# Attention stage of a two-layer perceiver block on one core: the out products of rows 0 to 511 are issued between the first softmax steps of rows 512 to 1023

## The reference

```
# _L0_attn_ref, on b=16, t=64, 16 heads
scores = einsum('bhqd,bhkd->bhqk', q, k) * scale
attn = softmax(scores + causal_mask)
out = einsum('bhqk,bhkd->bhqd', attn, v)
x = x + out @ wo + bo
# _L0_ffn_ref
xr = mu_r * x + (1 - mu_r) * x_prev ; xk = mu_k * x + (1 - mu_k) * x_prev
r = sigmoid(xr @ W_r) ; k = square(relu(xk @ W_k))
x = x + r * (k @ W_v)
```

## Time and profile before

| what | value |
|---|---|
| runs | 1480.25, 1472.99, 1463.63 us |
| profiled execution, time | 1465.62 us |
| its span | 1463.8 us, granted TensorE clock 0.959 on average |
| PE busy | 1343.8 us, 92% |
| DVE busy | 923.2 us, 63% |
| ACT busy | 557.0 us, 38% |
| POOL busy | 496.7 us, 34% |
| PE on the chain of waits | 69% |
| DVE on the chain of waits | 23% |

### The profile page before, as it was taken

The page is one execution under the profiler, slowest core; times in us unless marked ns, Lnnn a source line. Parts: engine busy times, 40 slices in busy tenths (PEclk is TensorE's granted clock), DMA queues, the critical chain, the costliest instruction groups (busy, mean ns, idle before and its releaser), DMA issues.

```text
span 1463.8 us, 28428 instructions
## 1 busy us (share of the span) xinstructions
PE 1343.8 (92%) x11066; PEld 812.0 (55%) x11066; DVE 923.2 (63%) x2273; ACT 557.0 (38%) x1149; POOL 496.7 (34%) x424
## 2 busy tenths in 40 slices
PE   6889999999999999999999867989898999889998
PEld 3458888888874444444445445444444455655554
DVE  6858888888743323500667586585998366676761
ACT  3446777777762222000133225142314234233430
POOL 3003100000048335733416220154690049996300
PEclk9979999999999999999999977999999999779999
DMA  6111232211112111311101110021320001110000
GB/s 187 39 50 64 83 99 75 64 64 61 53 44 87 57 57 58 73 57 57 31 29 32 57 30 2 25 92 58 115 97 27 1 2 60 60 59 1 1 22 36
DMA packets 50429, 79.19 MB, mean 54 GB/s; under 512 B 13808, under 2 KB 14320, under 8 KB 50304
## 3 DMA queue, kind: packets, MB, share of 16 engines
q1 hardware_dynamic: 47296, 70.83, 15.2%
q0 software_dynamic: 1920, 6.29, 1.4%
q10 hardware_dynamic: 1088, 0.37, 0.1%
HBM read 75.38 MB, written 2.10 MB: 53 GB/s over the span
## 4 chain that ended last, share of the span: by engine, by line
PE 69%; DVE 23%; issue 4%; ACT 3%; DMA 1%; POOL 0%; DVEq 0%; POOLq 0%; ACTq 0%
PE psum L635 40%; PE psum L968 7%; PE psum L877 4%; PE psum L644 4%; PE psum L1292 4%; PE psum L867 2%; DVE big L2210 2%; PE psum L980 1%; DVE stats L2181 1%; PE psum L650 1%; DVE big L1969 1%; PE psum L860 1%; DVE nw L1947 1%; PE psum L1280 1%; DVE nw L1948 1%
## 5 line engine op out<-in xcount | busy, mean ns | idle before, releaser
L2958 POOL TENSOR_TENSOR ring_hi<-stage,small 128x512 bf16<-128x512 f32 x128 | 139.6, 1101 | 618.0 <-DVE big L2226 373.6
L635 PE MATMUL psum<-y_mem,ring_hi 128*128 128x512 bf16 x896 | 269.8, 383 | 6.0 <-issue 2.1
L635 PE MATMUL psum<-ring_hi,y_mem 128*128 128x512 bf16 x576 | 171.8, 385 | 5.9 <-DVE ring_lo L2539 3.3
L635 PE MATMUL psum<-y_mem,ring_lo 128*128 128x512 bf16 x448 | 171.1, 382 | 0.0
L1413 ACT ACTIVATE big<-psum 128x400 bf16<-128x400 f32 (+2 forms) x232 | 124.2, 547 | 79.8 <-PE psum L635 40.0
L635 PEld LDWEIGHTS psum<-y_mem,ring_hi 128*128 (+1 forms) x896 | 87.0, 99 | 108.2 <-issue 8.7
L2961 POOL TENSOR_TENSOR ring_lo<-stage,ring_hi 128x512 bf16<-128x512 f32 x96 | 118.2, 1231 | 0.0
L635 PE MATMUL psum<-ring_lo,y_mem 128*128 128x512 bf16 x352 | 116.7, 383 | 1.2 <-DVE ring_lo L2651 1.2
L1413 ACT ACTIVATE y_mem<-psum 128x512 bf16<-128x512 f32 x64 | 37.0, 596 | 175.6 <-PE psum L644 175.2
L635 PEld LDWEIGHTS psum<-ring_hi,y_mem 128*128 128x128 bf16 x576 | 56.8, 99 | 71.9 <-issue 7.4
L2308 DVE TENSOR_TENSOR side<-psum,ybuf 128x512 f32<-128x512 f32 x32 | 22.1, 692 | 107.1 <-ACT ybuf L1640 107.1
(11 more groups left out here) (261 smaller groups left out, 2883.3 us busy)
## 6 DMA issues: line engine op xcount, KB each, us to landing
big<-in_ctx_dram SPq DMA_DIRECT2D x64, 200.0 KB
stage<-in_L_xattn_Wff_dram SPq DMA_DIRECT2D x12, 1024.0 KB, 5.3
ybuf<-in_L_ffn_W_fc_dram SPq DMA_DIRECT2D x16, 256.0 KB, 2.7
ybuf<-in_L_ffn_W_proj_dram SPq DMA_DIRECT2D x16, 256.0 KB, 2.9
stage<-in_L_ffn_W_fc_dram SPq DMA_DIRECT2D x4, 1024.0 KB, 5.3
stage<-in_L_ffn_W_proj_dram SPq DMA_DIRECT2D x4, 1024.0 KB, 5.4
stage<-in_L_xattn_Wout_dram SPq DMA_DIRECT2D x3, 1024.0 KB, 5.2
stage<-in_L_attn_W_qkv_dram SPq DMA_DIRECT2D x3, 1024.0 KB, 5.2
```

Of the source, the lines that this page charges most:

```text
L635: ins = pe.matmul(bank, l, r, start=n == 0, stop=n == len(passes) - 1)
L2958: pool.tensor_tensor(hi[:, k], src[:, k], zero, ALU.add).then_inc(pool_part, 1)
```

## The change

Two things change. In the main program, on PE, ACT and DVE alike, the softmax of half 1 is opened ahead of the rest of `attn_out(0, 0)`; its first four steps are issued one by one with the four out products between them, and only its last eight steps have three steps of `rest` behind each. The filler of 20 ahead of the out products is gone, and one of 24 stands behind the last softmax step. On POOL the split of a piece is issued as hi, lo, hi, lo, each with a wait for the one before, where it was hi, hi, lo, hi, lo, hi, lo, lo with waits on the piece before.

```diff
@@ PE @@
-            filler(0, 20)
-            run(ending)
-            abreast(soft(0, 1), rest, 3, False)
+            softmax = soft(0, 1)
+            abreast(itertools.islice(softmax, 4), ending, 1)
+            abreast(softmax, rest, 3, False)
+            filler(0, 24)
             run(rest)
@@ POOL, split @@
                     for k in range(KC):
                         pool.tensor_tensor(hi[:, k], src[:, k], zero, ALU.add).then_inc(pool_part, 1)
-                        if k:
-                            pool.wait_ge(pool_part, parts[0] + k)
-                            pool.tensor_tensor(lo[:, k - 1], src[:, k - 1], hi[:, k - 1], ALU.subtract)
-                    parts[0] += KC
-                    pool.wait_ge(pool_part, parts[0])
-                    pool.tensor_tensor(lo[:, KC - 1], src[:, KC - 1], hi[:, KC - 1], ALU.subtract).then_inc(pool_split, 1)
+                        parts[0] += 1
+                        pool.wait_ge(pool_part, parts[0])
+                        ins = pool.tensor_tensor(lo[:, k], src[:, k], hi[:, k], ALU.subtract)
+                        if k < KC - 1:
+                            ins.then_inc(pool_part, 1)
+                            parts[0] += 1
+                            pool.wait_ge(pool_part, parts[0])
+                    ins.then_inc(pool_split, 1)
+                    pool.wait_ge(pool_split, e + 1)
```

## The result

| | before | changed |
|---|---|---|
| median | 1470.69 us, 20 runs | 1462.64 us, 20 runs |
| profiled execution: time, span | 1465.62, 1463.8 us | 1463.5, 1461.7 us |
| granted TensorE clock, mean | 0.959 | 0.959 |
| POOL busy | 496.7 us | 502.5 us |

The changed kernel is faster: ratio 0.9959, 95% interval 0.9941 to 0.9978, so 6 us of 1470 with an interval of 3 to 9 (the medians are 8 apart). Forecast were 1466 us and a gain of 3.5. In the two profiled executions the spans differ by only 2.1 us, and this is not because the stage gained so little. The kernel before was profiled in one of its faster executions (1465.62 us against a median of 1470.69), the changed one close to its median. The stretches of the stage, cut at the events that bound the prediction's three parts: end of tile 4's exponential, start of `weigh` of tile 6, first mixing step, end of the squares.

A forecast was written before the change was run, and what follows sets the result against it. The prediction took a chain of waits to bound the kernel, carried almost everywhere by TensorE and mostly by VectorE otherwise. Stage -4.7, removed filler +1.0, POOL's order +0.2 gave -3.5 from 1469.3: 1466 us, range 1452 to 1479.

The forecast's parts named there:

- Part one: Four softmax steps of half 1 with the four out products, 828.5 to 846.1: 17.6 us.
- Part two: Eight softmax steps with 24 steps of `rest`, 846.1 to 893.9: 47.8 us, including +1.7 for the root beside Wqi's split.
- 52.2 - 6.1: Middle stretch before, 52.2 us, less 6.1 us of VectorE's softmax work, giving 46.1 us before the root's +1.7.
- Part three: Tail from first mixing step to end of squares: 27.6 us against 33.6, new filler of 24 lying in a 6.8 us wait.
- The removed filler: Filler of 20 ahead of the out products: its loss leaves 2.6 us idle and a lower clock, +1.0 us, bounds 0 to 3.4.
- POOL's order: POOL's splits each 0.8 us longer on 8.4, mostly off the chain: +0.2 us, between -2 and +3.
- The shift carries through: Everything after the stage hangs on it by semaphores, so its gain reaches the end: 1465.62 would become 1462.1 us.
- the first (-9, clock): Rival: TensorE is denser and its clock stays up, up to 5 us more gain: -9, 1460 us; chance 0.15.
- The second (nothing): Rival: waits in part one cost as much as the out products, or a later wait loses the gain: 1469; chance 0.15.
- the third: Rival: slower, late steps of `rest` bound the stage, first mixing step after 898: +8.6 with POOL, 1478; chance 0.15.
- The fourth (POOL's order on the path): Rival: POOL's order puts splits on the path in the feed-forward and folds: +12, 1481 us; chance 0.05.

The follow-up runs named there:

- e6: e1 with POOL's split of Wqi waiting until the norm's root is done; 1456.28 us, ratio 0.9909 against the kernel before.
- e3: The changed kernel without the new filler of 24 ahead of the gate products; 1465.11 us, ratio 0.9974 against the kernel before.
- e4: The changed kernel with the old filler of 20 put back ahead of the four softmax steps; 1465.31 us, ratio 0.9975 against the kernel before.
- e1: The changed kernel with POOL's split in its old order, new step order and filler edits kept; 1461.11 us, ratio 0.9979 against the kernel before.
- e2: The kernel before with only the new order of POOL's splits; 1466.12 us, ratio 0.9987 against the kernel before.
- e5: The changed kernel with POOL's old split order from the split of Wki on; 1458.67 us, ratio 0.9938 against the kernel before.
- e8: e1 with the filler ahead of the other half's gate products 34 long instead of 22; 1461.43 us, ratio 0.9975 against the kernel before.
- e7: e6 with two more splits, Wki's and the second attention's v, put behind VectorE's work; 1451.43 us, ratio 0.9897 against the kernel before.
- e10: e7 with Wki's split starting after 13 of the 16 mixing steps instead of 16; 1449.84 us, ratio 0.9851 against the kernel before.

## Why the prediction was right, and where it was not

**Part one** was exact: 17.6 us predicted, 17.6 measured, with the out products between the softmax steps and TensorE 17.19 us busy. On its way single steps were off by up to 0.4 us (the second exponential ends 10.5 us behind the first, 10.05 predicted), so the last tenth is luck.

**Part two** was 43.6 us instead of 47.8. One part of the miss is the root. I added 1.7 us to the 7.5 it took before, for eight held operations. Seven were held, and the root takes 7.7: 1.5 us too many, and the sum with six would have been nearer. The rule that I cited from the Trainium skill, "SBUF — State Buffer", section "Who interferes with whom", by which the two engines exclude each other for a whole instruction, agrees with the traces: with the split out of the way (e6) none of the thirteen is held. The other 2.7 us are in "52.2 - 6.1": I took off VectorE's work and left the stage's 11.2 us of VectorE idle as they were. They became 8.8 (43.6 less 34.82 busy). The stage's first half-clock stretch is 17.1 us (from 861.8) instead of 20.5, which fits, but which of the two brought the other isn't settled.

**Part three** was right: 27.9 us against 27.6, and so was its reason. The filler of 24 ran in 5.35 us and lay in the wait; the gates stayed at full clock, and without it (e3) they don't.

**The removed filler** was priced at +1.0 us and was a gain of 1.3 (e4). The idle of 2.6 us that I expected ahead of the transposes was 0.1 (825.89 to 825.97), since ACT was 2.6 us earlier against PE than in the earlier trace rows, and the clock is 1.00 from 825.9 to 843.5. The nearest row I had the earlier trace rows priced an idle that didn't come.

**POOL's order** was priced at +0.2 us, with -2 to +3 as bounds, and this is the step that hid most. It is a gain and a larger loss. Against e1 the changed kernel has 1.8 us less in S, and 1.3, 1.6 and 2.5 more in M, F and E; a split takes 9.3 us, as predicted (9.2). I had named the mechanism right ("catches one operation more, while each pause can let one through") and not the place that decides: four splits in a row, where every pause adds up, so that the last ends 1.4 us later beside VectorE's logic. In these two profiles that makes 3.6 us of net loss, more than my upper bound; between e2 and the kernel before, gain and loss cancel, and the medians tell neither. How much of M and E is POOL's isn't settled, and E differs by 2.5 us among kernels without later pauses; F is, by nine kernels.

**"The shift carries through"** failed in part. Of the stage's 8.4 us, M took back 3.1, F 1.7 and E 4.0; 2.5 us of lead were there before the stage began, and they are not the change's: e1, which has the kernel before's instructions up to there, leads by 2.2. That makes the 2.1 us of the spans. E1 and e5 gave up 3.4 us of 6.6 and 3.7 of 8.4. Most of M's part is the half clock at 965.77, since the gate products take 12.9 us to the `fold` instead of 10.4: with the longer filler (e8) the half clock is gone and M is 23.2, against 24.4 in e1. So I was wrong in the amount of the stage (-3.5 where it was -8.4) and in the rest (0 where it was +8.8 in this pair of profiles). The ratio's 6 us lie between: the number was near because two misses had opposite signs, and that is luck. Of the signs that I named, the first mixing step came at 887.1 and not at 892 to 894, the squares ended at 915.0 and not at 921 to 923; 2.5 us of either are the lead from before the stage.

Of the **rivals**, the first (-9, clock) had the size right for the stage, and the filler's 2.4 us are its mechanism. The second (nothing) is out by the interval, though what it named, a gain lost in later waits, is what took back 8.8 us in these profiles. For the third the first mixing step had to start after 898; it started at 887.1. The fourth (POOL's order on the path) happened on a small scale, and not in the feed-forward, where I had put it.

## What to carry to other kernels

Work of one engine that stands alone can be issued step for step between the steps of a stage that waits on another: four out products of 10.4 us gained 6.6 us in the stage that way, fillers included (e1), and its first part could be forecast by following each tile's chain engine by engine. After such a gain look at the next places where TensorE idles for microseconds, because there the clock can take it back: here 3.1 and 1.7 us of 8.4 were lost in the stretches with such places. And chains of small VectorE operations want POOL quiet: starting one split 11 us later (e6) gained 5.4 us in the stage, against 6.6 from the step order (e1).

## What the runs showed of the hardware

- Beside a split of eight POOL operations, VectorE operations of 0.16 us mostly take 0.7 to 1.1. In the root, with a dependent wait between POOL's operations (0.1 us), every second one gets through at 0.15 to 0.17; without it six in a row are held (before), or seven of eight (e1). `tensor_scalar` operations with one tile in SBUF can be held as well as those with two (0.89 us at 859.85), but need not be: beside the unpaused split of e1, from 1083.6 to 1088, four of them took 0.15 to 0.16 us between held operations of 1.0.
- The large steps are held too: mixing steps take 1.41 to 1.53 us beside a split, 0.75 without. Without the split (e7) the first gate product comes 3.4 us earlier. POOL loses there too: beside e1's mixing steps its operations take 1.48 and 1.60 us instead of 1.04 and 1.15.
- The idle alone does not tell whether the clock falls. Ahead of the gates the changed kernel and e7 both idled 2.55 and 2.56 us; the first stayed at full clock, the second had 3.4 us at half. All of e1, e6, e7, e8 and e10, with POOL's old order, had such a stretch there, and the changed kernel, e4 and e5, with the new one, had none. Why is open. The row of e7:

```profile
888.08 0.59 PE L635 MATMUL psum<-ring_hi,big 128*128 128x512 bf16 x1 [2.56 <-issue]
```
